# Twice the beats for the projections to queries and keys, and later turns of an attention group, in a woven four-layer transformer kernel

## The reference

```python
# layer 0, self: windows of 128      scores = q k / 4; softmax; times v
q, k, v = h @ w_qkv + b_qkv
# layer 0, context: top 16 of 77
q = h @ w_q + b_q
...
# layer 2, self, all tokens, masked
q, k = _apply_rope(q, cos, sin), _apply_rope(k, cos, sin)
a = softmax(where(mask, q k / sqrt(16), min)); out = a v
# layer 2 and 3, context: softmax over 77 keys
# layer 3, self, all tokens
```

## The kernel before

| phase | first lane | other lane | beats |
|---|---|---|---|
| 1 | modulation of layer 0 | norm, k, q, v of entry 0 | 7, 45 |
| 2 | window attention of entry 0 | norm, k, q, v of entry 1, modulation for experts | 81, 52 |
| 3 | window attention of entry 1 | projection, norm, q of entry 0, context keys | 81, 52 |
| 4 | top 16, first quarter | projection, norm, q of entry 1, modulations of layers 2 and 3 | 80, 52 |
| 5 | top 16, the rest | MLP and experts | 208, 268 |
| 6 | MLP | experts | 151, 105 |
| 7 | mask, norm, k, q (rotary), v of entry 0, context keys | experts | 68, 105 |
| 8 | full attention, layer 2, entry 0 | experts, norm, k, q (rotary), v of entry 1 | 363, 152 |
| 9 | full attention, layer 2, entry 1 | projection, norm, q, context attention, MLP, norm, k, q, v of entry 0 | 363, 265 |
| 10 | full attention, layer 3, entry 0 | the same for entry 1, and context keys | 307, 282 |
| 11 | full attention, layer 3, entry 1 | projection, norm, q, context attention, MLP of entry 0 | 307, 221 |
| 12 | projection to output for block 0 of entry 1 | the same for block 1 | 129, 129 |

## Time and profile before

### The profile page before, as it was taken

One profiled execution on the slowest core, in us unless ns is written; L12 is line 12 of the kernel. 1 busy time (PEld: TensorE's weight loads), 2 busy tenths in 40 slices (PEclk: granted clock), 3 DMA queues, 4 the chain that ended last, 5 costly groups with the idle time before them and its releaser, 6 DMA issues.

```text
span 2953.9 us, 37129 instructions
## 1 busy us (share of the span) xinstructions
PE 2453.4 (83%) x13127; PEld 1253.9 (42%) x13127; DVE 1806.5 (61%) x5631; ACT 1252.9 (42%) x2346; POOL 258.2 (9%) x252
## 2 busy tenths in 40 slices
PE   5777568787798878999788989987889978899678
PEld 2555325454455444444344445442234332234335
DVE  5554857677433466557667666648776667775344
ACT  2323324343222213445335555534646626666334
POOL 2010010010210010000020010010010010000201
PEclk8798689788899887999899999997999989999869
DMA  4545232000000130000232110042220032110120
GB/s 157 153 133 153 74 112 70 12 20 13 8 7 18 43 92 1 23 22 13 88 90 76 34 28 12 12 128 72 60 43 12 33 91 81 41 26 8 56 56 15
DMA packets 151646, 161.30 MB, mean 55 GB/s; under 512 B 33471, under 2 KB 120979, under 8 KB 151197
## 3 DMA queue, kind: packets, MB, share of 16 engines
q1 hardware_dynamic: 151460, 158.94, 18.6%
HBM read 98.04 MB, written 60.19 MB: 54 GB/s over the span
## 4 chain that ended last, share of the span: by engine, by line
PE 61%; DVE 21%; ACT 6%; DMA 5%; issue 3%; POOL 2%; SPq 2%; DVEq 0%; ACTq 0%; POOLq 0%
PE bank L1097 9%; PE bank L1560 7%; PE bank L1069 7%; PE bank L1044 7%; PE bank L1581 5%; PE bank L2034 3%; PE bank L1073 3%; PE bank L722 3%; DVE max L1170 3%; PE bank L1480 2%; PE bank L2211 2%; DVE bank L1167 2%; ACT work L1111 2%; PE bank L663 1%; PE bank L2036 1%
## 5 line engine op out<-in xcount | busy, mean ns | idle before, releaser
L1111 ACT ACTIVATE work<-bank 128x512 f32<-128x512 f32 (+1 forms) x1216 | 700.0, 597 | 631.7 <-PE bank L1073 283.9
L1167 DVE CUSTOM_DVE_ANT_0 bank<-bank,weights 128x512 f32<-128x512 f32 x512 | 349.1, 702 | 199.3 <-PE bank L1044 197.8
L1044 PE MATMUL bank<-k_stack,q_stack 97*128 97x512 bf16 x896 | 368.1, 414 | 79.6 <-DVE max L1167 36.3
L1170 DVE TENSOR_REDUCE max<-bank 128x1 f32<-128x512 f32 x512 | 340.5, 685 | 133.8 <-PE bank L1044 132.0
L1069 PE MATMUL bank<-q_stack,k_stack 99*128 99x512 bf16 x896 | 348.0, 391 | 17.1 <-ACT work L1111 13.9
L1560 PE MATMUL bank<-hT,weights 128*128 128x512 f32 x512 | 265.7, 618 | 17.7 <-ACT work L1606 6.5
L1073 PEld LDWEIGHTS bank<-ident_b,weights 128*128 128x128 bf16 x2048 | 161.1, 99 | 122.5 <-issue 16.3
L1044 PEld LDWEIGHTS bank<-k_stack,q_stack 97*128 97x128 bf16 x896 | 90.6, 101 | 282.7 <-DVE max L1167 107.1
L1073 PE MATMUL bank<-ident_b,weights 128*128 128x128 bf16 x2048 | 202.0, 221 | 0.0
L1581 PE MATMUL bank<-weights,work 128*128 128x256 f32 x768 | 196.4, 384 | 1.0 <-DVE work L1634 1.0
L663 PE MATMUL bank<-ident,work 128*128 128x128 f32 x320 | 84.8, 375 | 118.5 <-DVE work L641 113.1
(11 more groups left out here) (238 smaller groups left out, 3674.0 us busy)
## 6 DMA issues: line engine op xcount, KB each, us to landing
q_stack<-parts_q SPq DMA_DIRECT2D x60, 384.0 KB, 3.7
parts_q<-parts SPq DMA_DIRECT2D x46, 384.0 KB, 2.5
k_stack<-parts_k SPq DMA_DIRECT2D x40, 384.0 KB, 4.7
weights<-parts_q SPq DMA_DIRECT2D x36, 384.0 KB, 3.6
parts_q<-parts SPq DMA_DIRECT2D x46, 256.0 KB, 2.9
parts_k<-parts SPq DMA_DIRECT2D x24, 384.0 KB, 2.5
parts_k<-parts SPq DMA_DIRECT2D x24, 256.0 KB, 2.9
weights<-in_L_e_w SPq DMA_DIRECT2D x12, 512.0 KB, 5.6
```

Source lines behind the costliest of these rows:

```text
L1044: m = pe.e.matmul(bank.ap[:, :], self.q(g)[0:MAX_ROW, h, qt * P:(qt + 1) * P], k_stacks[self.key, g].ap[0:MAX_ROW, h, half * BLK:(half + 1 ...
L1111: ac.e.activation(p.ap[0:self.nk, :], banks[self.key, "exp", g, i].ap[0:self.nk, :], ACT.Exp).then_inc(*probs.tick((self.key, g, i)))
L1167: ve.e.tensor_tensor_reduce(bank[:, :], bank[:, :], mask_bias[:, qt, half * BLK:(half + 1) * BLK], 1.0, -3.4e38, ALU.add, ALU.max, to).the ...
L1170: ve.e.tensor_reduce(to, bank[:, :], AX_X, ALU.max).then_inc(*maxima.tick((self.key, g, i)))
```

## The change

Parts gets 4 beats an item instead of 2, and 4 more instead of 2 more around them (20 instead of 10 for 4 items). On PE two beats stand after the first of an item's two matmuls and two after the second. On DVE the operations are spread: in a rotary item shuffle and sine in one beat, add and cast in the next, subtract and cast in the third, the last subtract in the fourth; in a plain item subtract, cast, subtract in three beats. The turn of a group moves from one beat after ACT's copy to three (in the context kind, where a group has 8 beats, that is from beat 7 of a period to beat 1 of the next), its division with it, and attention gets two more beats at its end. The transpose of the rows and what follows it move one beat later in the full kind alone. In TopK the turn and the division move two beats later too.

The beats of the two lanes become: phase 1 7, 65; 2 83, 72; 3 83, 62; 4 82, 62; 5 210, 268; 6 151, 105; 7 88, 105; 8 365, 172; 9 365, 297; 10 309, 314; 11 309, 233; 12 137, 137. So a stage beside a first lane covers fewer of that lane's beats where Parts stands in its own lane: the norm before the last k and q of phase 9 stands at beats 285 to 305 of the first lane instead of 301 to 323, the k and q behind it at 305 to 354 instead of 323 to 351.

```diff
@@ class Parts
-                self.beats = 2 * len(self.items) + 2
+                self.beats = 4 * len(self.items) + 4
@@ tensor
                         if i == 0:
                             yield
+                            yield
                     m.then_inc(*dense.tick(k))
+                    yield
                     yield
@@ scalar
-                    yield
+                    yield from rest(3)
@@ pool
+                yield from rest(4)
                 for c, bl in self.items:
-                    yield
-                    yield
...
+                    yield from rest(4)
@@ vector
+                yield from rest(4)
                 for c, bl in self.items:
-                    yield
-                    yield
...
                         ve.e.tensor_tensor(r.ap[:, :], r.ap[:, :], sinT, ALU.mult).then_inc(*vec.tick((k, "sin")))
+                        yield
...
                         ve.e.tensor_copy(p.ap[:, 0, :], t).then_inc(*vec.tick((k, "p0")))
+                        yield
                         ve.wait_ge(*vec[k, "p0"])
...
                     ve.e.tensor_tensor(t, t, p.ap[:, 0, :], ALU.subtract).then_inc(*vec.tick((k, "r1")))
+                    if not self.rope:
+                        yield
                     ve.wait_ge(*vec[k, "r1"])
                     ve.e.tensor_copy(p.ap[:, 1, :], t).then_inc(*vec.tick((k, "p1")))
+                    yield
                     ve.wait_ge(*vec[k, "p1"])
                     ve.e.tensor_tensor(p.ap[:, 2, :], t, p.ap[:, 1, :], ALU.subtract).then_inc(*vec.tick((k, "p2")))
+                    yield from rest(1 if self.rope else 2)
@@ class Attention
-                self.beats = lead + period * (self.groups - 1) + self.fin_at + 4
+                self.beats = lead + period * (self.groups - 1) + self.fin_at + 6
+                self.rows_lag = 2 if kind == "full" else 1
@@ sync, tensor, vector
-                    if now := self.group(beat, self.rows_at + 2, 1):
+                    if now := self.group(beat, self.rows_at + self.rows_lag + 1, 1):
...
-                    if now := self.group(beat, self.rows_at + 1, 1):
+                    if now := self.group(beat, self.rows_at + self.rows_lag, 1):
...
-                    if now := self.group(beat, self.fin_at + 1, 1):
+                    if now := self.group(beat, self.fin_at + 3, 1):
...
-                    if now := self.group(beat, self.fin_at + 2, 1):
+                    if now := self.group(beat, self.fin_at + 4, 1):
@@ class TopK
-                self.beats = self.lead + self.period * self.groups + 11
+                self.beats = self.lead + self.period * self.groups + 13
...
-                    if now := self.group(beat, 22, 1):
+                    if now := self.group(beat, 24, 1):
...
-                    if now := self.group(beat, 23, 1):
+                    if now := self.group(beat, 25, 1):
```

## The result

The changed kernel takes 2971.6 us (median of four runs, 2969.0 to 2973.5), the kernel before beside it 2945.7: a ratio of 1.0072, with a 95% interval from 1.0051 to 1.0094. It is slower; I had forecast 2919, with a range up to 2946, and called faster 0.80. Its profiled execution is 2969.0 us, its span 2967.7.

What follows compares the result with a forecast made beforehand. PE was taken to bound the kernel where it has work, DVE where its queue holds PE up. Gains -49, costs +18 and +4 given back sum to -27: 2928.3 us profiled, less 9.0, 2919; range 2893 to 2946.

Steps and rivals of the forecast that it cites:

- A: Rotary items in phase 8: spread over more beats, they level DVE's work with PE's; -17 us, between -22 and -9.
- B: Rotary items in phase 7: DVE's backlog, for which PE waits at the experts' activation, goes; -8 us, between -12 and 0.
- Rival 1: DVE stays the bound in phase 8, so gains shrink; 2932 to 2941 us, chance 0.16.
- rival 4: In phase 7 the add still stands right behind the sine, so B is 0; 2927 us, counted within the forecast's 0.52.
- C: Turns: two beats later, PE's 24.7 us of waits for ACT's copy shrink; -11 us, between -20 and -3.
- D: Rows in full attention: one beat later covers most of 9.5 us of PE's waits; -6 us, between -9 and 0.
- rival 3: Waits move and don't shrink, and stretched items cost as much as they free; 2941 to 2952 us, chance 0.09.
- E: Window attention: with later turns, waits for the division and for maxima shrink; -4 us, between -8 and 0.
- F: Plain items in phases 9 to 11: some of the 38.2 us L1044 waits for L1170 go; -3 us, between -5 and 0.
- H: Phase 3 into 4: later context keys' loads stand ahead of phase 4's query load; +3 us, between 0 and +6.
- G: Context turns, phases 9 to 11: added wait in bank 5, 0.3 to 0.8 us a group; +7 us, between 0 and +18.
- rival 2: Bank 5: context turns wait for a DVE backlog, 2 us more for each of 24 groups; 2960 us, chance 0.09.

Runs made afterwards that it cites:

- e4: Kernel before with four beats an item only in the four rotary stages (layer 2's queries and keys, phases 7 and 8), nothing else changed: ratio 0.9905.
- e11: Kernel before with the turn of full attention alone three beats behind its copy, rows untouched: ratio 1.0022.
- e8: Kernel before with full attention's turn three beats behind its copy and its rows one beat later; context, window and top 16 untouched: ratio 1.0043.
- e12: Kernel before with the rows of full attention alone one beat later, turns untouched: ratio 0.9993.
- e6: Kernel before with four beats an item in the four rotary stages and the window groups' turn alone three beats behind its copy: ratio 0.9855.
- e1: Kernel before with only the Parts half of the change (four beats an item); turns, rows and top-16 stage as before: ratio 0.9943.
- e7: Kernel before with the context turn alone three beats behind its copy instead of one: ratio 1.0111.
- e5: Changed kernel with one thing undone, the context turn again one beat behind its copy: ratio 0.9985.
- e10: e7 with the context's exponential's scores, product and copy one beat later, the turn left in its place in bank 5: ratio 1.0078.
- e9: e7 with the context turn in bank 7, the bank of the sums, instead of bank 5: ratio 1.0028.
- e14: e6 with the context turn at its old place, one beat behind the copy, but in bank 7 instead of bank 5: ratio 0.9816.
- e2: Kernel before with only the later turns, full attention's later rows and later top-16 turns; Parts at two beats an item: ratio 1.0043.

## Why the prediction was wrong

- **A and B, right.** -17 and -8 were forecast, the profile of e4 has -15 and -10, and its ratio makes 28 us in all. In the changed kernel the stretch around the rotary keys runs at 44.6 and 43.6 us for 40 beats each, the 1.1 us a beat that I named, at 0.96 and 0.92 where the earlier trace rows has 0.77; in phase 7 L2219, the line that was L2211, waits 0.2 us, not 10.9:

```profile
1372.20:1416.80 44.60, 40.26 (x281) 18.16 (x278) 36.89 (x98) 21.55 (x37) 7.09 (x4) 0.96 0.31 95
1416.80:1460.40 43.60, 38.66 (x266) 17.39 (x263) 29.13 (x73) 20.95 (x37) 7.09 (x4) 0.92 0.38 122
```

```profile
DVE work L779 <- POOL work L759: 8.9, 7, 1.6
...
PE bank L2219 <- DVE work L2241: 0.2, 1, 0.2
```

  POOL's wait of 8.9 us stands as foreseen. Rival 1 (DVE stays the bound) and rival 4 don't hold.
- **C, D in full attention, failed steps.** Here I counted a wait that goes as time that goes. The wait for the copy did go (24.7 to 2.4). The turn in full attention lost 0.2% all the same (e11): part of its wait came back at the rows, as rival 3 has it, and what idle time did go was more than paid for by a lower granted clock, which I had not priced (7 us less idle, 17 more busy in its profile). -17 was forecast for C and D together, of which I put some -10 on full attention; +13 was measured there (e8, 1.0043), +6 with the turn alone (e11). D by itself, -6 forecast and -2 measured (e12), can't be told from right; but where it let only first groups feel the later rows, full attention's own wait for the rows' DMA (L1077 for q_stack<-max_parts) grew from 6.0 to 10.7 us.
- **E, mis-sized.** The mechanism was there, but -4 measured as -15 (e6 against e4). Of the 20 us by which phases 2 and 3 are shorter in e6, 9 are busy time on the same matmuls at a higher granted clock, and I priced idle time alone.
- **F, H, I, J, nearly right as a sum.** +8 forecast, about +11 measured (e1 over e4, give or take 13). F's gain did not come. H shows in the 13.0 us of L1251, where L1243 has 6.6: 6.4 for the +3 that I gave it, though the earlier end of the window's phase has its share in that (e6).
- **G, the step that turned the sign.** +7 forecast, +33 measured (e7; 23 to 42 by its interval), 1.4 us for each of 24 groups, the very point from which rival 2 decides; inside the change it is 26 us (e5). But rival 2's mechanism, the turn waiting for a backlog of DVE, is not there: in phases 9 to 11 L925 waits 0.8 us at most and 6.6 in all. My price of the turn's own wait was right, at the low end. What failed is that I took everything else around the turn as unchanged. The time that the old turn and its waits took had covered the rows' DMA, for which PE now waits 17 us; what that costs in time, 0.3% by e10, is not clear of noise. And the turn is a sixth user in eight beats of bank 5, which has four tiles and the rows to serve: taking it out brings 0.8% where it stands now and 0.4% where it stood (e9, e14). The difference, the price of the new place, is about as large as its uncertainty. In e7's profile the waits for the DMA, the maximum and the division grow by 19 us and that for the copy shrinks by 5, which is about what this execution is over the profile before (14 us). It was the fastest of five, and what the others lose beyond that no trace shows.
- **The sum.** By the runs: rotary -28, window -15, full +13, context +33, plain +11, together +14 us; the change measured +21. That the two are near is luck. Window, full and context alone add up to +31, but e2, which has all three, measured +13; and over e1 the same half costs 38 us. The parts don't add: one difference of some -18 us, at the edge of the intervals, and one of +25, outside them, nearly cancel, and no run says where the second comes from. My range reached to 2946 because I took rival 2 for one long wait that could be excluded, and gave 0.09 to a sum of short ones.
- **The rule of the Trainium skill** ("SBUF — State Buffer", Who interferes with whom) that I weighed, a DVE instruction with two inputs in SBUF against a GpSimd instruction that reads SBUF, did not come up. The masked maximum, one of whose inputs is in PSUM, takes 0.70 us in both kernels and 0.74 at most, the cosine 1.77 us in both. The gain of A and B, which such a lock on the maxima would have taken, came in full.

## What to carry to other kernels

Before a step is moved, ask what it covers where it stands: a transfer that lands behind it will be waited for. Count the occupants of each PSUM bank in a period, and give a step that turns up between two others of a single bank a bank that is idle at that time; here that edit was worth 0.4% with the turn in its old place, 0.8% with the turn moved and 1.5% in the changed kernel. A wait that is gone from the list is not yet time gained: look for who waits in its place, and at what clock the rest runs. A beat added to one stage of a woven lane is taken from all its neighbours, so stretch only the stage that holds the others up.

## What I had not expected of the hardware

A short hole costs more than its length when the clock falls behind it. In the changed kernel PE is idle for 0.60 and 1.25 us around a turn; the same matmul before and after takes 0.38 and 0.64 us, and the five us that follow run at a granted clock of 0.50, that is at 1.2 GHz:

```profile
2083.00:2090.00 7.00, 5.90 (x38) 1.64 (x36) 4.39 (x11) 3.70 (x7) 0.00 (x0) 1.00 0.15 31
2090.00:2093.00 3.00, 1.22 (x7) 0.59 (x6) 2.00 (x6) 1.35 (x3) 0.00 (x0) 0.97 0.36 124
2093.00:2098.00 5.00, 4.93 (x22) 1.41 (x22) 2.35 (x5) 2.38 (x4) 0.00 (x0) 0.50 0.21 72
```

Not every such pair does it: in e7, with the same order of the context's instructions and much the same waits, the stretch of this attention stayed at 0.99. Nor does it need the change: in the kernel before, six us behind the holes of 0.89 and 1.26 us shown above run at 0.72:

```profile
2092.00:2098.00 6.00, 5.67 (x34) 1.88 (x35) 3.32 (x8) 3.00 (x6) 0.00 (x0) 0.72 0.01 3
```

Over the phases that got longer, 9 to 12, PE's idle time grew by 24 us and its busy time on the same matmuls by 27.
